# Mamba layer with feed-forward: two scan products on VectorE, each with an operand in PSUM, in place of GpSimd

## The reference

```
cs = jnp.cumsum(a, axis=-1)
Ldec = jnp.where(tri, jnp.exp(cs[..., :, None] - cs[..., None, :]), 0.0)
Xdt = Xc * dtc[..., None]
att = jnp.einsum('bchqn,bchkn->bchqk', Cc, Bc) * Ldec
Yd = jnp.einsum('bchqk,bchkp->bchqp', att, Xdt)
dec_end = jnp.exp(cs[..., -1:] - cs)
states = jnp.einsum('bchq,bchqn,bchqp->bchpn', dec_end, Bc, Xdt)
g = jnp.exp(cs[..., -1])
def step(S, inp):
    gk, st = inp
    return (gk[:, :, None, None] * S + st, S)
Yo = jnp.einsum('bchqn,bchpn,bchq->bchqp', Cc, prev, jnp.exp(cs))
```

## Time and profile before

| | |
|---|---|
| median of 3 runs | 493.44 us (492.25 to 493.79) |
| the profiled execution | 491.24 us, its span 489.5 us |
| granted TensorE clock over the span, mean | 0.998 |
| busy: TensorE / VectorE / ScalarE / GpSimd | 472.6 / 312.1 / 236.5 / 206.7 us |
| the scan | from 45 to 155 us of the span |

### The profile page before, as it was taken

How to read it: one execution, slowest core, us unless ns; L and a number is a source line. 1 busy time by engine, 2 the same in 40 slices (tenths; PEclk the granted TensorE clock), 3 DMA queues, 4 the chain that set the end, 5 groups by cost and what they waited for, 6 DMA issues and landing times.

```text
span 489.5 us, 6236 instructions
## 1 busy us (share of the span) xinstructions
PE 472.6 (97%) x2112; PEld 377.4 (77%) x2112; DVE 312.1 (64%) x534; ACT 236.5 (48%) x444; POOL 206.7 (42%) x236
## 2 busy tenths in 40 slices
PE   7998999999999899999999899999999999999995
PEld 7876777776777678888788778888888888888884
DVE  3793676745787766677988989866948523411233
ACT  5887767776567765645233344224815530032300
POOL 6834464525662687676787000010014342133321
PEclk9999999999999999999999999999999999999999
DMA  8532021012213324442333066411300000200001
GB/s 247 206 109 68 20 86 66 21 44 105 89 46 126 109 77 160 153 171 98 110 116 116 16 239 212 147 46 37 98 16 1 0 1 12 75 1 0 2 17 68
DMA packets 14431, 40.80 MB, mean 83 GB/s; under 512 B 2368, under 2 KB 2368, under 8 KB 14400
## 3 DMA queue, kind: packets, MB, share of 16 engines
q1 hardware_dynamic: 14400, 40.41, 24.2%
HBM read 38.30 MB, written 2.10 MB: 83 GB/s over the span
## 4 chain that ended last, share of the span: by engine, by line
PE 83%; DVE 9%; issue 3%; ACT 3%; POOL 2%; POOLq 0%; DVEq 0%
PE psA L1622 8%; PE psA L1623 8%; PE psA L1409 6%; PE psA L1411 6%; PE psB L1632 4%; PE psB L1631 4%; PE psA L1415 3%; PE psA L1417 3%; PE psA L1597 3%; PE psA L1601 3%; PE psA L1600 3%; DVE xbc L1164 3%; PE psB L1597 3%; PE psB L1600 2%; PE psB L1601 2%
## 5 line engine op out<-in xcount | busy, mean ns | idle before, releaser
L1622 PE MATMUL psA<-xT_h,q_gu 128*128 128x512 f32 x176 | 70.1, 398 | 0.0
L1623 PE MATMUL psA<-xT_l,q_gu 128*128 128x512 f32 x176 | 69.1, 392 | 0.0
L667 POOL TENSOR_SCALAR var<-mv 128x1 f32<-128x1 f32 x16 | 4.9, 304 | 128.7 <-DVE mv L1056 128.6
L1027 ACT ACTIVATE gate_t<-psA 128x512 f32<-128x512 f32 x22 | 13.1, 597 | 75.1 <-PE psA L1623 75.1
L1361 DVE TENSOR_TENSOR prod_t<-gate_t,psA 128x512 f32<-128x512 f32 x22 | 15.1, 688 | 51.7 <-PE psA L1623 48.6
L812 POOL TENSOR_TENSOR int_l<-prod_t,int_h 128x512 fp32r<-128x512 f32 x22 | 28.7, 1304 | 45.7 <-ACT int_h L1032 45.7
L729 POOL TENSOR_TENSOR beta<-wsum,beta 128x512 fp32r<-128x512 f32 x28 | 36.0, 1309 | 24.8 <-ACT beta L888 24.8
L1622 PEld LDWEIGHTS psA<-xT_h,q_gu 128*128 128x128 f32 x176 | 33.1, 188 | 8.2
L1623 PEld LDWEIGHTS psA<-xT_l,q_gu 128*128 128x128 f32 x176 | 33.1, 188 | 7.4
L1632 PE MATMUL psB<-q_dn,int_l 128*128 128x512 f32 x88 | 34.3, 389 | 0.0
L1631 PE MATMUL psB<-q_dn,int_h 128*128 128x512 f32 x88 | 34.2, 389 | 0.0
(11 more groups left out here) (253 smaller groups left out, 1348.0 us busy)
## 6 DMA issues: line engine op xcount, KB each, us to landing
raw<-in_f_gu_t SPq DMA_DIRECT2D x22, 512.0 KB, 3.4
raw<-in_w_gu_t SPq DMA_DIRECT2D x14, 512.0 KB, 4.1
raw<-in_f_dn_t SPq DMA_DIRECT2D x10, 512.0 KB, 3.5
raw<-in_w_gu_t SPq DMA_DIRECT2D x14, 256.0 KB, 2.6
raw<-in_w_dn_t SPq DMA_DIRECT2D x7, 512.0 KB, 3.4
raw<-in_w_in_t SPq DMA_DIRECT2D x5, 512.0 KB, 4.0
x<-in_hidden SPq DMA_DIRECT2D x8, 256.0 KB, 4.7
out<-x SPq DMA_DIRECT2D x8, 256.0 KB, 2.0
```

Source lines behind the costliest of these rows:

```text
L1622: nc.tensor.matmul(ps, w, seq(xT_h, k, b), start=k == 0, stop=False)
L1623: done = nc.tensor.matmul(ps, w, seq(xT_l, k, b), start=False, stop=k == KD - 1)
```

## The change

The products `xs` and `ecs` move from GpSimd to VectorE, and each reads one operand from PSUM. `xs` reads x from bank `xb` itself, not from the copy `xnbn`; for c < 3 it is VectorE's product, and no longer ScalarE's copy, that frees the bank, and VectorE waits for its end (`v.wait_ge(*freed_b(("xb", b, c)))`) before the `decay` update. ScalarE writes Exp of `csb` back into its bank; VectorE multiplies that bank by C into `ecs`, behind the `decay` update, and frees it. Before, ScalarE freed it after Exp. GpSimd keeps `decay` plus `diag_d`. TensorE waits for `b_free` of `xb` and of `csb` in place of `xs_ready` and `cs_scaled`.

```diff
--- before.py
+++ after.py
@@ -430,8 +430,8 @@
         xbc_ready = sem("xbc_ready")
         gend_ready = sem("gend_ready")
         wend_ready = sem("wend_ready")
-        xs_ready = sem("xs_ready")
-        cs_scaled = sem("cs_scaled")
+        xnbn_ready = sem("xnbn_ready")
+        ecs_ready = sem("ecs_ready")
         yth_done = sem("yth_done")
         y_ready = sem("y_ready")
         u_ready = sem("u_ready")
@@ -769,26 +769,6 @@
                 elif kind == "decay":
                     b, c = at
                     t = NC * b + c
-                    if c < NC - 1:
-
-                        i = (NC - 1) * b + c
-                        pool.wait_ge(wend_ready, i + 1)
-                        pool.wait_ge(*freed_b(("xb", b, c)))
-                        if i >= 1:
-
-                            before = (b, c - 1) if c else (b - 1, NC - 2)
-                            pool.wait_ge(*done_b(("st", *before)))
-                        nc.gpsimd.tensor_tensor(heads(xs[:]), xnbn[:, 0:P].unsqueeze(1).to_broadcast([P, H, P]),
-                                                wend[:, t % 2, :].unsqueeze(2).to_broadcast([P, H, P]), ALU.mult)\
-                            .then_inc(xs_ready, 1)
-                    if c > 0:
-
-                        i = (NC - 1) * b + c - 1
-                        pool.wait_ge(*freed_b(("csb", b, c)))
-                        pool.wait_ge(xbc_ready, NX * (b + 1))
-                        nc.gpsimd.tensor_tensor(heads(ecs[:]), heads(ecs[:]), xbc[b][:, 2:NX, chunk(c)], ALU.mult)\
-                            .then_inc(cs_scaled, 1)
-
                     pool.wait_ge(*freed_b(("cb", b, c)))
                     pool.wait_ge(diag_ready, 1)
                     nc.gpsimd.tensor_tensor(decay[:], decay[:], diag_d[:], ALU.add).then_inc(att_ready, 1)
@@ -946,8 +926,9 @@
                     if t >= 1:
 
                         s.wait_ge(*done_b(("y", (t - 1) // NC, (t - 1) % NC)))
+
                     nc.scalar.activation(xnbn[:], bank_b(("xb", b, c))[:, 0:2 * P], ACT.Copy)\
-                        .then_inc(freed_b(("xb", b, c))[0], 1)
+                        .then_inc(xnbn_ready if c < NC - 1 else freed_b(("xb", b, c))[0], 1)
 
                     s.wait_ge(*done_b(("seg", b, c)))
                     nc.scalar.activation(decay[:], bank_b(("seg", b, c)), ACT.Exp)\
@@ -959,7 +940,7 @@
                         nc.scalar.activation(gend[:, t % 2, :], heads(bank_b(job))[:, :, P - 1], ACT.Exp)\
                             .then_inc(gend_ready, 1)
                         s.wait_ge(gend_ready, (NC - 1) * b + c)
-                        nc.scalar.activation(ecs[:], bank_b(job), ACT.Exp).then_inc(freed_b(job)[0], 1)
+                        nc.scalar.activation(bank_b(job), bank_b(job), ACT.Exp).then_inc(ecs_ready, 1)
                 elif kind == "state":
                     t = tile_of(step)
                     s.wait_ge(*freed_b(("y", *at)))
@@ -1176,12 +1157,18 @@
                     v.wait_ge(dt_ready, b + 1)
                     if c < NC - 1:
                         i = (NC - 1) * b + c
-                        if i >= 2:
-
-                            v.wait_ge(xs_ready, i - 1)
                         nc.vector.tensor_tensor(wend[:, t % 2, :], heads(decay[:])[:, :, P - 1],
                                                 dtT[:, b, H * c:H * c + H], ALU.mult).then_inc(wend_ready, 1)
                         v.wait_ge(wend_ready, i + 1)
+                        v.wait_ge(xnbn_ready, i + 1)
+                        if i >= 1:
+                            last = (b, c - 1) if c else (b - 1, NC - 2)
+                            v.wait_ge(*done_b(("st", *last)))
+                        nc.vector.tensor_tensor(
+                            heads(xs[:]), bank_b(("xb", b, c))[:, 0:P].unsqueeze(1).to_broadcast([P, H, P]),
+                            wend[:, t % 2, :].unsqueeze(2).to_broadcast([P, H, P]), ALU.mult)\
+                            .then_inc(freed_b(("xb", b, c))[0], 1)
+                        v.wait_ge(*freed_b(("xb", b, c)))
                     job = ("cb", b, c)
                     v.wait_ge(*done_b(job))
                     for h in range(H):
@@ -1189,6 +1176,14 @@
                             out=decay[:, chunk(h)], in0=decay[:, chunk(h)], scalar=dtT[:, b, H * c + h:H * c + h + 1],
                             in1=bank_b(job)[:, chunk(h)], op0=ALU.mult, op1=ALU.mult)
                     last.then_inc(freed_b(job)[0], 1)
+                    if c > 0:
+                        i = (NC - 1) * b + c - 1
+                        job = ("csb", b, c)
+                        v.wait_ge(ecs_ready, i + 1)
+                        if i >= 1:
+                            v.wait_ge(*done_b(("y", b, c - 1) if c > 1 else ("y", b - 1, NC - 1)))
+                        nc.vector.tensor_tensor(heads(ecs[:]), heads(bank_b(job)), xbc[b][:, 2:NX, chunk(c)], ALU.mult)\
+                            .then_inc(freed_b(job)[0], 1)
                 elif kind == "state":
                     b, c = at
                     t = NC * b + c
@@ -1519,15 +1514,13 @@
                     t = NC * b + c
                     pe.wait_ge(*freed_b(("xb", b, c)))
                     if c < NC - 1:
-
-                        pe.wait_ge(xs_ready, (NC - 1) * b + c + 1)
                         ps = open_b(("st", b, c))
                         nc.tensor.matmul(ps, xnbn[:, P:2 * P], xs[:], start=True, stop=True).then_inc(b_done, 1)
 
                     ps = open_b(("y", b, c))
                     if c > 0:
                         pe.wait_ge(*freed_b(("st", b, c - 1)))
-                        pe.wait_ge(cs_scaled, (NC - 1) * b + c)
+                        pe.wait_ge(*freed_b(("csb", b, c)))
                         for h in range(H):
                             nc.tensor.matmul(ps[:, chunk(h)], state[:, (c - 1) % 2, chunk(h)],
                                              ecs[:, chunk(h)], start=h == 0, stop=False)
```

## The result

The changed kernel takes 497.48 us (median of 4 runs, 497.35 to 497.84) and the kernel before 492.96 us (4 runs, 492.25 to 493.79): a ratio of 1.009, 95% interval 1.0073 to 1.0106, so it is 4.5 us slower. The forecast was 497.4. The profiled execution after took 497.35 us, its span 495.6 us, at a mean granted clock of 0.997.

What follows compares the result with a forecast made beforehand. TensorE, busy 97% of the span, was taken as the bound. Terms 2.65 + 1.4 + 0.24 - 0.34 = +3.95 us, on the median of 493.44, gave 497.4 us; range 495.0 to 499.4 (main forecast alone 496.4 to 498.4).

Steps and rivals of the forecast that it cites:

- The price of the instruction: Each new VectorE product reading a PSUM bank takes 0.69 us, like yt, within bounds of 0.68 and 1.12 us.
- Rival E: VectorE's new product costs the upper bound, 1.12 us: +1.3 us at three places and 0.4 at (1,0), 499.1 us; chance 0.05.
- `outproj(1,0)`: TensorE waits for the bank of xb of (1,1), held until VectorE's xs behind alpha and wend: +2.65 us.
- the 0.7 us at the `y` matmul of (1,0): xs and decay update now in a row on VectorE, GpSimd's addition 0.7 us later; counted at nothing, 0.8 us of slack.
- `turn2(1,0)`: Waits for the bank of xb of (1,2): 1.59 us late, 0.20 back at once at outproj(1,1), net +1.4 us.
- `outproj(0,0)`: Waits for the bank of xb of (0,1), held until VectorE's xs ends: +0.24 us.
- The recovery in (1,3): TensorE's seg follows cb sooner, since GpSimd without its products finishes until_l before xT_l: -0.34 us.
- B: TensorE's later waits for act and psB give the shift back: +0.1 us, 493.5; half, +2.2 us, 495.6; chance 0.07 within 0.3%.
- C: Not slower, xs of (1,1) not late at its bank: -0.7 us, 492.7; chance 0.04, and 0.03 for over 0.3% faster.
- D: TensorE's granted clock falls behind the new waits, making the kernel slower; size not given in the text; chance 0.05.

Runs made afterwards that it cites:

- the order experiment: Changed kernel with each decay step of batch 1 moved ahead of the load ga step it stood behind: 493.07 us, ratio 1.0009 to the kernel before.
- the run from the copy: Changed kernel, but xs on VectorE reads the SBUF copy xnbn and ScalarE's copy frees the bank of xb as before: 494.79 us, ratio 1.0044.
- the last kernel above: Kernel before with ecs alone on VectorE, batch 1 decay ahead of load ga, and the state copy of (1,0) ahead of the load step: 491.53 us, ratio 0.9977.
- the other kernel: Kernel before with GpSimd's xs freeing the bank of xb, plus unread transposes, 16 ahead of outproj(1,0) and 10 ahead of turn2(1,0): 498.56 us; without transposes 500.31 us.

## Why the prediction was right, step by step

**The price of the instruction** was 0.69 us; it is 0.691 and 0.684. Rival E is out.

**`outproj(1,0)`, forecast +2.65 us**: the shift grows from 2.11 at `outproj(0,0)` to 4.76, by 2.65. The slot after `alpha` and `wend` is where it was put, and the order experiment removes the wait by moving that slot alone. Inside it, the 0.7 us at the `y` matmul of (1,0), which was counted at nothing, does show (1.41 us of wait instead of the earlier trace rows's 0.34, less the 0.37 us ahead of `st` that are gone because `xs` is done sooner), and is covered as the prediction said. With the bank no longer held it comes out of that cover: it is one part of what the run from the copy kept.

**`turn2(1,0)`, forecast +1.59 and -0.20**: measured +1.69 (4.76 to 6.45) and -0.17.

**`outproj(0,0)`, forecast +0.24 us: the term was too small**, 0.65 in all (1.46 to 2.11). Its own mechanism gives about 0.24; the other 0.42 arises before it, by `seg` of (0,1), +1.88. VectorE's short instructions on dt, in the timeline of the changed kernel with GpSimd beside them:

```profile
52.15 1.28 POOL L774 TENSOR_TENSOR decay<-decay,diag_d 128x512 f32<-128x512 f32 x1 [3.85 <-DVE decay L1175]
53.39 1.04 POOL L741 TENSOR_TENSOR until_h<-tri,adt_h 128x512 fp32r<-128x512 bf16 x1
54.39 1.04 POOL L741 TENSOR_TENSOR until_l<-tri,adt_l 128x512 fp32r<-128x512 bf16 x1
```
```profile
52.49 0.98 DVE L1118 SCALAR_TENSOR_TENSOR dtw<-dtw 128x16 f32<-128x16 f32 x1
53.89 0.57 DVE L1121 TENSOR_SCALAR dtw<-dtw 128x16 f32<-128x16 f32 x1 [0.42 <-ACT dtw L904]
54.49 0.96 DVE L1124 SCALAR_TENSOR_TENSOR dtw<-dtw 128x16 f32<-128x16 f32 x1
55.49 0.17 DVE L1126 TENSOR_SCALAR dtw<-dtw 128x16 f32<-128x16 f32 x1
```

`xs` ahead of the `decay` update makes GpSimd's addition start later, so that its three operations run beside these instructions for longer. Lines 1124 and 1118 take 0.96 and 0.98 us where the kernel before has 0.18 and 0.23 for the same two (it pays for the overlap too, but less: line 1121 takes 0.83 us there and 0.57 here), and both end with a GpSimd operation: 54.49 + 0.96 = 55.45 and 54.39 + 1.04 = 55.43; 52.49 + 0.98 = 53.47 and 52.15 + 1.28 = 53.43. From line 1121 to the copy of `state` that frees the bank of `seg`, the chain took 2.74 us before (52.43 to 55.17) and takes 3.16 now (53.89 to 57.05): the 0.42. The Trainium skill (SBUF — State Buffer, "Who interferes with whom") says that a VectorE instruction with two inputs in SBUF contends with a GpSimd instruction that reads SBUF; these two are of that kind and the trace agrees. That these 0.42 us hang on this was read from the traces, and no run here isolated it.

**The recovery in (1,3), forecast -0.34 us: too large**, it is -0.11 (6.28 to 6.17). The matmul of `seg` does start earlier, as the earlier trace rows suggested, but in the kernel before the matmul behind it followed after 0.34 us (140.13 to 140.47), where here the same step is 0.6 us wide. A matmul that has waited starts late and is followed closely, so a recovery must be read from the matmul behind it.

The two errors, +0.41 and +0.23, with the 0.13 at `turn2` and behind it, make 4.71 out of the forecast 3.95 (4.72 with rounding). The cost was 0.8 us too small by the traces and 0.6 by the medians; that the forecast of 497.4 is nearer than that is chance: it was built on the median of 493.44, and the larger samples of the kernel before have 492.67 to 492.86.

**The rivals.** B, the later waits absorb the shift: both are there with 2.1 and 1.8 us, later by the shift; it is out. C: the bank of (1,1) was late. By the Trainium skill (GPSIMD Engine Reference, "4.1 Engine selection") VectorE was the better place; the run with `ecs` alone shows nothing measurable from it, and for `xs` it costs time as long as the product stands behind the load step. D, the clock, was given 0.05 and an argument from one row. In the changed kernel it stayed at 1.00 around the 1.72 us wait. But the mechanism is real, and nearer than I had put it: a wait of 2.85 us had it in one profiled execution, whose time one of the other three shares, and a wait of 3.49 us had it in the profiled one, with a mean clock of 0.991 or less in all four. The forecast priced D at the same place for a delay of 2.6 us, and one stretch with gaps and a full clock was thin evidence against it.

## What to carry to other kernels

When a product takes over a PSUM operand, ask first who frees the bank and what stands ahead of it in that engine's program order; the speed of the engine comes after that. Here 0.69 us instead of 1.04 cost 4.5 us, and moving the step in front of an unrelated load gave back 4.1. When several engines' steps come from one list, undo such a loss by moving the step, and look what the step that was passed is now late for (0.88 us here). And price a wait of TensorE of some microseconds by its length plus a possible drop of the clock behind it.

## What the runs showed of the hardware that I had not expected

**TensorE's clock also falls behind waits that the kernel before has.** In the profiled execution of the last kernel above, behind the wait of 1.8 us for `act`, the windows are:

```profile
168.00:171.00 3.00, 1.21 (x5) 0.86 (x5) 1.29 (x4) 2.71 (x6) 2.02 (x2) 0.93 0.03 10
171.00:175.00 4.00, 4.00 (x13) 3.16 (x12) 1.09 (x2) 1.63 (x3) 3.92 (x6) 0.62 0.00 0
```

The kernel before has 1.00 in both windows of its profiled execution, with the same wait and the same 1.21 us busy. The drop costs 1.4 us at first (the shift goes from -0.35 at 171.24 to +1.01 at 172.87), but most of that comes back at the next wait, which the late TensorE no longer has. The kernel before, and then the last kernel:

```profile
179.85 0.47 PE L1409 MATMUL psA<-tT_h,a 128*128 128x512 f32 x1 [0.84 <-DVE psB L1258]
```
```profile
179.94 0.39 PE L1423 MATMUL psA<-tT_h,a 128*128 128x512 f32 x1
```

Between 170.44 and 181.09 the shift goes from -0.47 to -0.01, so 0.5 us stay. Five of the thirteen profiled executions (that of 963 us left out) have this drop, and 0.5 us stay in each. Three (one of them among the five) have one behind the wait for `xbc` at 45 us, and there the whole 1.6 us stay: in the run from the copy the shift is 1.95 at 50.51 and 1.97 at 105.76. Of the 17 executions of the kernel before in the last set seven, at a mean clock of 0.997 or 0.998, took 491.10 to 492.27 us, and ten, at 0.992 to 0.995, took 492.66 to 493.78. That the ten had such drops is likely and was not seen, as only one execution was profiled; at which wait, and how much of the difference is the start-up, is open. The Trainium skill (TensorE: Matmul & The Clock Gate, "HAM oscillation — how this bites in real kernels") describes a matmul engine that runs slower behind waits; the runs here agree, and show that the same wait does it in some executions and not in others.

**Idle work can pay.** 34 transposes that nobody reads save 2.6 us (500.93 against 503.51). With 26 of them the four executions of the other kernel reach to 498.68 us and not to 502.34, where two of the four without them stayed at 498.5 as well.
